# A four-tap convolution whose newest tap is written by ScalarE from the projection's bank

## The chip, the cores and the metric

The kernel runs on one core of a Trainium2 chip. The metric is the time of one execution on the device in microseconds; a kernel is given by the median of its runs. Two lengths are used: the time of a run, and the span of its profile from the first to the last instruction.

## The reference

The input is x of 32 sequences, 256 positions and 256 features, and a context of 120 keys for each sequence. Six blocks follow one another, each as x = layernorm(x + block(x)): random features, cross attention over the context with 16 heads, a gated rotation network with three cycles, a state space block, a gated product with the context, and a router over 8 experts. The state space block is the one that the change touches:

```python
xr = x @ W_in.T
x_ssm, res = (xr[..., :inner], xr[..., inner:])          # inner = 512
xc = jnp.pad(jnp.transpose(x_ssm, (0, 2, 1)), ((0, 0), (0, 0), (K - 1, 0)))
xc = lax.conv_general_dilated(xc, conv_w, (1,), 'VALID', feature_group_count=inner, ...)   # K = 4
x_conv = silu(jnp.transpose(xc, (0, 2, 1)) + conv_b)
delta = softplus(x_conv)
A_d = jnp.exp(delta[..., None] * -jnp.exp(A_log))         # 16 states
h = a_t * h + bx_t[..., None]; y = c_t * jnp.sum(h, axis=-1)   # over the sequence, bx = x_conv ** 2
return (y_ssm * silu(res) + D * x_conv) @ W_out.T
```

The convolution is depthwise and causal: output position s is the sum over k = 0 to 3 of conv_w[k] times input position s - 3 + k. Tap k = 3 is the newest one; it reads the position itself and needs no padding.

## The kernel before

The 32 sequences go in 16 groups of two (G = 16, NB = 2), that is 512 positions on the free axis. Three groups are in work at a time. In one turn of the loop the function `turn` (TensorE) or `turn_` (the other engines) does the front of group f (attention, then the rotation network), the state space block of group m = f - 1, the back of group b = f - 2 (gated product, router, experts), and prepares f + 1. The order of instructions on every engine is written out by hand, and each engine works through its own list strictly in that order; semaphores tie the lists together. Fifteen turns have both an f and an m, 14 of them a b too; in the last turn with an m there is no f.

The state space block starts with a projection of 1024 outputs in 8 chunks of 128 (`mamba_in`). TensorE writes chunks 0, 2, 4 and 7 to bank 4, chunks 1, 3 and 5 to bank 5, chunk 6 to bank 7 (`IN`). Chunks 0 to 3 are the convolution's input, chunks 4 to 7 are `res`. TensorE mixes the chunks with other work in this order: chunks 0 and 1, the queries of f, chunk 2, scores 0, chunk 3, scores 1, the turned x of b, chunk 4, scores 2, the gated product's input, scores 3, chunk 5, scores 4, chunk 6, scores 5 to 7, chunk 7, and then the attention itself. The scores rotate over three banks, and two groups of them stand in front of VectorE's maxima at the most: a group waits for the semaphore `smax_ready` of the group before it.

ScalarE (`mamba_in`, L1437) copies each of chunks 0 to 3 from its bank to `xpad`, a tile in SBUF with three zero columns ahead of each sequence, and raises `in_read`; TensorE waits for `in_read` before it fills a bank again. ScalarE's order around this is: the turned x of f and m, chunks 0 and 1, the queries of f, chunks 2 and 3, the turned x of b (`x45T`), a load of the silu table, silu of convolution chunks 0 and 1, softplus of them, six decays, silu of chunks 2 and 3, and then `res` (L1440).

VectorE computes the convolution from `xpad` in two calls (`convolve(m, 0)` and `convolve(m, 2)`), two chunks each. A call waits for both of its chunks. Tap 0 is a TENSOR_SCALAR (L1064), which writes `conv`; taps 1 to 3 are SCALAR_TENSOR_TENSOR (L1066), which add to it. The two chunks alternate, so that an instruction waits for the one before the last. VectorE's order is: the norm of b, `convolve(m, 0)`, four maxima of the scores (L991), `convolve(m, 2)`, twelve maxima, and then the scans (L1087) with everything else between them. The tile `conv` is the same memory as `soft` and `delta`: softplus is written over it, GpSimd adds to it (L1658), and ScalarE's 64 decays (L1479) read it.

GpSimd adds up the 16 states of each chunk (L1671) while VectorE scans.

Of the kernel before, what the change touches and what calls it, by code (L numbers as in the profile page):

```python
# [21 lines left out]
ALU = mybir.AluOpType  # L22
ACT = mybir.ActivationFunctionType
# [3 lines left out]
B, S, D = 32, 256, 256  # L27
# [10 lines left out]
INNER, STATES, TAPS = 512, 16, 4  # L38
IC = INNER // P
# [97 lines left out]
def program(nc, ins, out):  # L137
    nc.disable_value_cache = True
    with ExitStack() as ctx:
        def sb(name, shape, dt=F32):  # L140
            return ctx.enter_context(nc.sbuf_tensor(name, shape, dt))

        def sem(name, per=1, head=0):
            return Signal(ctx.enter_context(nc.semaphore(name)), per, head)

        def chain(name, per):
            return Chain(ctx.enter_context(nc.semaphore(name)), per)
# [6 lines left out]
        def col(name, k=0, rows=P):  # L154
            at = COLUMNS[name][0] + k
            return W["columns"][0:rows, at:at + 1]
# [70 lines left out]
        xpad = sb("xpad", [P, IC, NB, PAD + S])  # L227
# [3 lines left out]
        conv = delta = soft  # L231
# [108 lines left out]

        in_psum = sem("in_psum", 2 * IC)
        in_read = sem("in_read", 2 * IC)
        conv_chain = chain("conv_chain", IC * (TAPS - 1))
        conv_ready = sem("conv_ready", IC)
        xc_ready = sem("xc_ready", IC)
        exp_ready = sem("exp_ready", IC)
# [84 lines left out]
        IN = [bank[k][:, :] for k in (4, 5, 4, 5, 4, 5, 7, 4)]  # L431
# [101 lines left out]
        def _(pe):  # L533
            def mm(o, l, r, start, stop):
                return pe.matmul(o, l, r, start=start, stop=stop)  # L535
# [188 lines left out]
            def mamba_in(g, b, j0, j1):  # L724
                if j0 == 0:
                    if g == 0:
                        pe.wait_ge(loaded_rest.sem, 16 * len(REST))
                    pe.wait_ge(n3.xT_ready.sem, n3.xT_ready.at(g, DC))
                for j in range(j0, j1):
                    if j == IC + 2:  # L730
                        if b is not None:
                            pe.wait_ge(n4.xT_ready.sem, n4.xT_ready.at(b, DC))
                    elif j >= 2:
                        pe.wait_ge(in_read.sem, in_read.at(g, IC + 1 if j == 2 * IC - 1 else j - 1))
                    for c in range(DC):
                        last = mm(IN[j], winT[:, c, j * P:(j + 1) * P], n3.xT[:, c, :], c == 0, c == DC - 1)
                    last.then_inc(in_psum.sem, 1)
# [80 lines left out]
            def turn(f, m, b, nxt):  # L818
# [7 lines left out]
                if m is not None:  # L826
                    norm_turn(pe, n3, m, TURN)
                    mamba_in(m, b, 0, 2)
                if f is not None:
                    queries(f)  # L830
                if m is not None:
                    mamba_in(m, b, 2, 3)
                if f is not None:
                    scores(f, 0, 1)
                if m is not None:
                    mamba_in(m, b, 3, 4)
# [100 lines left out]
        def _(v):  # L937
# [113 lines left out]
            def convolve(g, c0):  # L1051

                if c0 == 0:
                    conv_chain.start(v, g)
                v.wait_ge(in_read.sem, in_read.at(g, c0 + 2))
                for k in range(TAPS):
                    for c in range(c0, c0 + 2):
                        o = conv[:, c, :].rearrange("p (b s) -> p b s", b=NB)
                        x = xpad[:, c, :, k:k + S]
                        w = col("conv_w", c * TAPS + k)  # L1060
                        if k:
                            conv_chain.settle(1)
                        if k == 0:
                            step = v.tensor_scalar(o, x, w, None, ALU.mult)  # L1064
                        else:
                            step = v.scalar_tensor_tensor(out=o, in0=x, scalar=w, in1=o, op0=ALU.mult,  # L1066
                                                          op1=ALU.add)
                        if k < TAPS - 1:
                            conv_chain.then(step)
                        else:  # L1070
                            step.then_inc(conv_ready.sem, 1)
                            if c == c0:
                                conv_chain.settle()
                if c0 + 2 == IC:
                    conv_chain.end()
# [147 lines left out]
            def turn_(f, m, b, nxt):  # L1223
# [4 lines left out]
                if m is not None:  # L1228
                    convolve(m, 0)
                if f is not None:  # L1230
                    maxima(f, 0, 2)
                if m is not None:
                    convolve(m, 2)
# [103 lines left out]
        def _(a):  # L1337
# [95 lines left out]
            def mamba_in(g, j0, j1):  # L1433
                for j in range(j0, j1):
                    a.wait_ge(in_psum.sem, in_psum.at(g, j + 1))
                    if j < IC:
                        a.copy(xpad[:, j, :, PAD:PAD + S], IN[j].rearrange("p (b s) -> p b s", b=NB))\  # L1437
                            .then_inc(in_read.sem, 1)
                    else:
                        a.activation(res[:, j - IC, :], IN[j], ACT.Silu).then_inc(in_read.sem, 1)  # L1440
# [68 lines left out]
            def turn_(f, m, b, nxt):  # L1509
# [7 lines left out]
                if m is not None:  # L1517
                    mamba_in(m, 0, 2)
                if f is not None:
                    queries(f)  # L1520
                if m is not None:
                    mamba_in(m, 2, IC)
# [250 lines left out]
```

## Time and profile before

| | before |
|---|---|
| median of 3 runs | 3107.59 us |
| lowest and highest run | 3103.23 and 3112.39 us |
| the profiled execution, its time | 3099.29 us |
| the profiled execution, its span | 3097.5 us |
| TensorE busy (matmul) | 2540.1 us, 82% |
| VectorE busy | 2495.3 us, 81% |
| ScalarE busy | 1727.8 us, 56% |
| GpSimd busy | 1487.4 us, 48% |
| mean granted clock of TensorE | 0.872 |

Names in the profile: PE is TensorE's matmuls, PEld its weight loads, DVE VectorE, ACT ScalarE, POOL GpSimd. A line L1066 is line 1066 of the kernel; `mm` is a helper at L535, so nearly all matmuls bear that line and are told apart by their tiles. Times in a timeline are microseconds from the start of the span. A timeline merges neighbouring instructions of one form: "x2" is two instructions, and the length beside it is that from the start of the first to the end of the last. Two neighbours overlap a little, so two of 0.59 us can take 1.07 us. The brackets at a row's end give the engine's idle time before it and what ended it.

### The profile page before, as it was taken

Reading aid. Unit: us, or ns where it says so; the run is one execution under the profiler, and the core shown is the slowest. Engines: PE = TensorE matmul, PEld = TensorE weight load, DVE = VectorE, ACT = ScalarE, POOL = GpSimd, SP = SyncE. Lnnn points to the kernel's source line nnn. Section 1 sums busy time; section 2 is a strip of 40 time slices with the busy share of each in tenths; the row PEclk is TensorE's granted clock in tenths of the full one; section 3 lists DMA queues with packets and bytes.
Section 4 is the critical chain, followed back from the end, with each engine's and each line's share of the span. In section 5 each row is a group of like instructions: output and inputs, shape, how many; then the busy total and the mean of one; then the engine's idle time right before and its main releaser. Section 6 shows DMA issues by size and latency. Waiting matters only on the chain.

```text
span 3097.5 us, 41602 instructions
## 1 busy us (share of the span) xinstructions
PE 2540.1 (82%) x11020; PEld 1469.9 (47%) x11020; DVE 2495.3 (81%) x4288; ACT 1727.8 (56%) x3062; POOL 1487.4 (48%) x1159
## 2 busy tenths in 40 slices
PE   6896888979888897888988788888888889887556
PEld 3544554544444454445545444554544445454323
DVE  2368888897978889898888978788897888978783
ACT  1457564646657474665646466564656646465620
POOL 1046354554535455563545545354553545456460
PEclk7868888888989989999898899898898989978687
DMA  3000000000000000000000000000000000000000
GB/s 131 10 8 10 14 11 14 17 14 7 10 21 10 14 17 14 7 10 21 10 14 13 18 7 10 21 10 14 13 3 21 10 14 7 7 7 1 14 7 7
DMA packets 16849, 45.72 MB, mean 15 GB/s; under 512 B 2248, under 2 KB 7056, under 8 KB 16400
## 3 DMA queue, kind: packets, MB, share of 16 engines
q1 hardware_dynamic: 16656, 43.96, 4.2%
q14 instruction: 171, 1.40, 0.2%
q8 instruction: 22, 0.36, 0.1%
HBM read 35.57 MB, written 8.39 MB: 14 GB/s over the span
## 4 chain that ended last, share of the span: by engine, by line
PE 47%; DVE 28%; issue 14%; ACT 7%; DVEq 2%; POOL 1%; ACTq 0%; DMA 0%; SPq 0%; POOLq 0%
PE bank L535 45%; DVE h_ring L1087 14%; DVE x L1199 3%; DVE ln_stats L387 2%; DVE smax L991 1%; POOL ysum L1671 1%; ACT a_ring L1479 1%; DVE x L405 1%; DVE xpad L1093 1%; PE bank L413 1%; DVE soft L1066 1%; ACT L1485 1%; ACT L1339 1%; DVE ln_mv L391 1%; ACT spare L1420 1%
## 5 line engine op out<-in xcount | busy, mean ns | idle before, releaser
L1671 POOL TENSOR_TENSOR ysum<-ysum,h_ring 128x512 f32<-128x512 f32 x896 | 1155.2, 1289 | 633.3 <-DVE h_ring L1087 571.3
L1087 DVE TENSOR_TENSOR_SCAN h_ring<-a_ring,bank 128x512 f32<-128x512 f32 x1024 | 1172.7, 1200 | 27.2 <-ACT bank L1474 16.2
L1479 ACT ACTIVATE a_ring<-soft,decay 128x510 f32<-128x510 f32 x1024 | 675.7, 717 | 198.4 <-DVE h_ring L1087 198.0
L535 PE MATMUL bank<-w_expert_w,x45T 128*128 128x512 f32 x1024 | 541.1, 675 | 199.0 <-DVE x L1199 191.4
L535 PEld LDWEIGHTS bank<-w_expert_w,x45T 128*128 128x128 f32 x1024 | 213.2, 216 | 490.9 <-DVE x L1199 253.5
L1658 POOL TENSOR_TENSOR soft<-xc,soft 128x512 f32<-128x512 f32 x64 | 81.0, 1276 | 655.2 <-ACT soft L1457 655.2
L535 PE MATMUL bank<-x3T,w_winT 128*128 128x512 f32 x512 | 291.0, 704 | 39.7 <-ACT x3T L419 31.4
L991 DVE TENSOR_REDUCE smax<-bank 128x4 f32<-128x480 f32 x256 | 156.4, 652 | 143.1 <-PE bank L535 143.1
L535 PE MATMUL bank<-qT,kmask 32*120 32x256 f32 x1024 | 207.2, 497 | 50.2 <-ACT spare L1386 40.6
L535 PE MATMUL bank<-spare,w_cn_w 128*128 128x256 f32 x768 | 217.7, 408 | 37.0 <-ACT spare L1416 22.4
L1199 DVE SCALAR_TENSOR_TENSOR x<-bank,weight,x 128x256 f32<-128x256 f32 x512 | 212.5, 474 | 40.4 <-PE bank L535 40.4
L398 ACT ACTIVATE ln_logv<-ln_mv,eps 128x4 f32<-128x4 f32 x96 | 28.3, 295 | 330.5 <-DVE ln_mv L391 252.7
L535 PE MATMUL bank<-kmask,qT 32*128 32x240 f32 x1024 | 151.8, 417 | 46.1 <-DVE smax L991 45.2
L1386 ACT ACTIVATE spare<-bank 120x512 f32<-120x512 f32 x256 | 138.4, 593 | 81.5 <-PE bank L535 81.4
L535 PEld LDWEIGHTS bank<-x3T,w_winT 128*128 128x128 f32 x512 | 104.3, 220 | 165.1 <-issue 111.5
L535 PEld LDWEIGHTS bank<-spare,w_cn_w 128*128 128x128 f32 x768 | 131.8, 193 | 105.7 <-ACT spare L1416 37.3
L535 PE MATMUL bank<-x12T,w_cn_w 128*128 128x256 f32 x768 | 180.0, 384 | 2.3 <-ACT x12T L1372 2.3
L1671 POOL TENSOR_TENSOR ysum<-h_ring 128x512 f32<-128x512 f32 x64 | 81.3, 1270 | 197.5 <-DVE h_ring L1087 197.5
L413 PE MATMUL bank<-w_ident,x 128*128 128x128 f32 x640 | 127.4, 322 | 49.6 <-DVE x L405 45.6
L535 PEld LDWEIGHTS bank<-x12T,w_cn_w 128*128 128x128 f32 x768 | 146.0, 192 | 40.3 <-issue 20.1
L1416 ACT ACTIVATE spare<-bank,w_columns 128x256 f32<-128x256 f32 x192 | 80.5, 472 | 139.6 <-PE bank L535 139.3
L535 PEld LDWEIGHTS bank<-kmask,qT 32*128 32x128 f32 x1024 | 94.9, 198 | 129.5 <-DVE smax L991 83.8
(149 smaller groups left out, 3890.2 us busy)
## 6 DMA issues: line engine op xcount, KB each, us to landing
x0T<-in_xT SPq DMA_DIRECT2D x16, 512.0 KB, 3.3
x<-in_x SPq DMA_DIRECT2D x16, 512.0 KB, 4.3
out<-x SPq DMA_DIRECT2D x16, 512.0 KB, 3.0
ctxT<-in_ctxT SPq DMA_DIRECT2D x16, 240.0 KB, 2.5
ctxTb<-in_ctxT SPq DMA_DIRECT2D x16, 240.0 KB, 2.7
ctxb<-in_ctx SPq DMA_DIRECT2D x16, 240.0 KB, 3.0
w_expert_w<-in_expert_w SPq DMA_DIRECT2D x1, 2048.0 KB
w_winT<-in_winT SPq DMA_DIRECT2D x1, 1024.0 KB
```

The lines of the kernel that those rows point to most:

```text
L387: n.chain.then(v.bn_stats(n.stats[:, t, :], n.sum[:, t, :]))
L391: last = v.bn_aggr(n.mv[:, t, :], n.stats[:, t, :])
L413: last = pe.transpose(banks[c][:, t * P:(t + 1) * P], n.x[:, t, c * P:(c + 1) * P], ident[:, :])
L535: return pe.matmul(o, l, r, start=start, stop=stop)
L991: v.tensor_reduce(smax[:, t, :].rearrange("p (e r h) -> p r e h", e=DC, r=4)[:, r, :, :], bank[u % 3][:, 0:480].rearrange("p (e h k) -> p ...
L1087: scanned.then(v.tensor_tensor_scan(h_ring[:, k % HRING, :], a_ring[:, k % RING, :, :].rearrange("p b s -> p (b s)"), xc2, 0.0, ALU.mult, ...
L1199: v.scalar_tensor_tensor(out=acc[:, t, :], in0=MB[s % 2][:, e * D:(e + 1) * D], scalar=weight[:, t, x:x + 1], in1=acc[:, t, :], op0=ALU.mu ...
L1386: a.activation(probs[:, s % 4, :, :].rearrange("p k s -> p (k s)"), bank[s % 3][0:KEYS, :], ACT.Exp, scale=1.0 / np.sqrt(DK)).then_inc(pro ...
L1416: a.activation(h1[:, b, r, :], bank[b][:, r * S:(r + 1) * S], ACT.Gelu, bias=col("cn_b1", r)).then_inc(l1_ready.sem, 1)
L1479: a.activation(a_ring[:, k % RING, :, 1:S], delta[:, c, :].rearrange("p (b s) -> p b s", b=NB)[:, :, 1:S], ACT.Exp, scale=decay[:, k:k + 1 ...
L1658: p.tensor_tensor(out=delta[:, c, :], in0=xc[:, c, :], in1=soft[:, c, :], op=ALU.add)\
L1671: p.tensor_tensor(out=total, in0=first, in1=h_ring[:, k % HRING, :], op=ALU.add)\
```

## The change

For chunks 0 to 3 ScalarE issues two reads of the bank instead of one. The first is new: it multiplies the bank by the weight of tap 3 (a column of 128 weights, one for each partition) and writes the result to the convolution's tile, raising the new semaphore `tap_ready`. The second is the copy to `xpad`, as before. VectorE waits for both, and adds taps 0, 1 and 2 with SCALAR_TENSOR_TENSOR; its TENSOR_SCALAR is gone. TensorE waits for `tap_ready` beside `in_read` before it fills a bank again. The taps are added in another order.

```diff
-        conv_chain = chain("conv_chain", IC * (TAPS - 1))
+        conv_chain = chain("conv_chain", IC * (TAPS - 2))
+        tap_ready = sem("tap_ready", IC)
...
                         pe.wait_ge(in_read.sem, in_read.at(g, IC + 1 if j == 2 * IC - 1 else j - 1))
+                        pe.wait_ge(tap_ready.sem, tap_ready.at(g, min(j - 1, IC)))
...
                 v.wait_ge(in_read.sem, in_read.at(g, c0 + 2))
-                for k in range(TAPS):
+                v.wait_ge(tap_ready.sem, tap_ready.at(g, c0 + 2))
+                for k in range(TAPS - 1):
                     for c in range(c0, c0 + 2):
                         o = conv[:, c, :].rearrange("p (b s) -> p b s", b=NB)
-                        x = xpad[:, c, :, k:k + S]
-                        w = col("conv_w", c * TAPS + k)
                         if k:
                             conv_chain.settle(1)
-                        if k == 0:
-                            step = v.tensor_scalar(o, x, w, None, ALU.mult)
-                        else:
-                            step = v.scalar_tensor_tensor(out=o, in0=x, scalar=w, in1=o, op0=ALU.mult,
-                                                          op1=ALU.add)
-                        if k < TAPS - 1:
+                        step = v.scalar_tensor_tensor(out=o, in0=xpad[:, c, :, k:k + S],
+                                                      scalar=col("conv_w", c * TAPS + k), in1=o, op0=ALU.mult,
+                                                      op1=ALU.add)
+                        if k < TAPS - 2:
                             conv_chain.then(step)
...
                     if j < IC:
+                        a.activation(conv[:, j, :], IN[j], ACT.Copy, scale=col("conv_w", j * TAPS + TAPS - 1))\
+                            .then_inc(tap_ready.sem, 1)
                         a.copy(xpad[:, j, :, PAD:PAD + S], IN[j].rearrange("p (b s) -> p b s", b=NB))\
                             .then_inc(in_read.sem, 1)
```

## Rows read from the trace of the kernel before

**Rows 1.** Page: busy time of each engine; the chain that ended last, by engine.

```profile
PE 2540.1 (82%) x11020; PEld 1469.9 (47%) x11020; DVE 2495.3 (81%) x4288; ACT 1727.8 (56%) x3062; POOL 1487.4 (48%) x1159
...
PE 47%; DVE 28%; issue 14%; ACT 7%; DVEq 2%; POOL 1%; ACTq 0%; DMA 0%; SPq 0%; POOLq 0%
```

**Rows 2.** Timeline of VectorE: start of the first convolution in two turns.

```profile
333.43 0.89 DVE L1064 TENSOR_SCALAR soft<-xpad,w_columns 128x512 f32<-128x512 f32 x2 [1.54 <-ACT xpad L1437]
...
2694.54 0.89 DVE L1064 TENSOR_SCALAR soft<-xpad,w_columns 128x512 f32<-128x512 f32 x2 [1.16 <-ACT xpad L1437]
```

**Rows 3.** Timeline of VectorE, one turn, both halves of the convolution.

```profile
1238.63 0.89 DVE L1064 TENSOR_SCALAR soft<-xpad,w_columns 128x512 f32<-128x512 f32 x2 [2.04 <-ACT xpad L1437]
1239.43 4.06 DVE L1066 SCALAR_TENSOR_TENSOR soft<-xpad,w_columns,soft 128x512 f32<-128x512 f32 x6
1244.16 1.22 DVE L991 TENSOR_REDUCE smax<-bank 128x4 f32<-128x480 f32 x2 [0.67 <-PE bank L535]
...
1248.23 0.87 DVE L1064 TENSOR_SCALAR soft<-xpad,w_columns 128x512 f32<-128x512 f32 x2
1249.02 4.06 DVE L1066 SCALAR_TENSOR_TENSOR soft<-xpad,w_columns,soft 128x512 f32<-128x512 f32 x6
1252.99 1.21 DVE L991 TENSOR_REDUCE smax<-bank 128x4 f32<-128x480 f32 x2
```

**Rows 4.** Timeline of TensorE: same turn; two rows of the first turn.

```profile
1241.24 1.88 PE L535 MATMUL bank<-x3T,w_winT 128*128 128x512 f32 x4
...
1244.06 1.98 PE L535 MATMUL bank<-x3T,w_winT 128*128 128x512 f32 x4
...
1253.70 1.08 PE L535 MATMUL bank<-kmask,qT 32*128 32x240 f32 x8 [0.97 <-DVE smax L991]
...
1263.19 1.97 PE L535 MATMUL bank<-kmask,qT 32*128 32x240 f32 x8 [0.74 <-DVE smax L991]
1265.09 3.78 PE L535 MATMUL bank<-x3T,w_winT 128*128 128x512 f32 x4
...
181.57 1.97 PE L535 MATMUL bank<-kmask,qT 32*128 32x240 f32 x8 [3.81 <-DVE smax L991]
```

**Rows 5.** Chain that ended last, same turn: start, length, what.

```profile
1234.27 12.83 PE bank L535 x40
...
1253.08 0.58 DVE smax L991
```

**Rows 6.** Groups by line and form: busy, mean ns; idle before, releaser.

```profile
L1066 DVE SCALAR_TENSOR_TENSOR soft<-xpad,w_columns,soft 128x512 f32<-128x512 f32 x192 | 129.9, 745 | 0.0
L1064 DVE TENSOR_SCALAR soft<-xpad,w_columns 128x512 f32<-128x512 f32 x64 | 28.1, 482 | 52.7 <-ACT xpad L1437 52.7
...
L1378 ACT ACTIVATE qT<-bank,w_columns 128x512 f32<-128x512 f32 x32 | 22.0, 688 | 37.2 <-PE bank L535 37.2
```

**Rows 7.** Timeline of ScalarE, same turn.

```profile
1238.01 0.59 ACT L1437 COPY xpad<-bank 128x512 f32<-128x512 f32 x1 [1.13 <-PE bank L535]
1239.73 0.69 ACT L1378 ACTIVATE qT<-bank,w_columns 128x512 f32<-128x512 f32 x1 [1.13 <-PE bank L535]
...
1246.08 0.59 ACT L1437 COPY xpad<-bank 128x512 f32<-128x512 f32 x1 [2.34 <-PE bank L535]
1247.68 1.08 ACT L419 COPY x45T<-bank 128x512 f32<-128x512 f32 x2 [1.01 <-PE bank L413]
...
1262.63 1.55 ACT L1440 ACTIVATE res<-bank 128x512 f32<-128x512 f32 x3
1268.90 0.60 ACT L1440 ACTIVATE res<-bank 128x512 f32<-128x512 f32 x1 [4.73 <-PE bank L535]
```

**Rows 8.** Timeline of ScalarE, last turn with a convolution.

```profile
2882.50 1.08 ACT L419 COPY x45T<-bank 128x512 f32<-128x512 f32 x2
```

**Rows 9.** Stretches: length, busy time of engines, granted clock, DMA share, GB/s.

```profile
1264.00:1266.00 2.00, 2.00 (x7) 0.93 (x6) 0.81 (x2) 0.17 (x1) 0.00 (x0) 0.50 0.00 0
```

**Rows 10.** Timeline of TensorE: chunks 0 and 1 in another turn.

```profile
693.74 6.78 PE L535 MATMUL bank<-x3T,w_winT 128*128 128x512 f32 x8 [2.49 <-ACT x3T L419]
```

## The prediction

> **What bounds the kernel now.** I read the page first. TensorE and VectorE are both busy a little over 80% of the span, ScalarE 56%, and the chain of work that ended last runs 47% over TensorE and 28% over VectorE, 7% over ScalarE [rows 1]. So no engine is full from end to end: the end is set by a path that changes engines, and a microsecond counts only where that path passes. I then took one turn of the loop out of the middle (1234 to 1414 us) and laid the engines' timelines beside each other. Fifteen turns have this shape (a group in the convolution stage and one in the score stage together); from the first convolution at 333.43 us to that at 2694.54 us there are 13 turn lengths, so 181.6 us each [rows 2].
>
> The convolution stands twice in a turn, and its two halves are unlike. The first half starts at 1238.63 us, when ScalarE has copied chunk 1, and ends at 1243.49; VectorE then idles 0.67 us for TensorE's first scores [rows 3]. The second half starts at 1248.23 us with no idle before it, ends at 1253.08, and the maxima behind it start at once [rows 3]. TensorE stands still for 0.97 us before the scores of 1253.70, and is released by the first of those maxima [rows 4]. The chain says the same: it goes straight through the second half, its first maximum and into TensorE, while at the first half it is on TensorE, one piece of 12.83 us [rows 5]. This release is in all 15 turns: 14 show a wait of 0.97 to 1.06 us at this place, the first turn one of 3.81 us [rows 4]. The last convolution (2879 us) has no scores beside it.
>
> **What is removed.** Four TENSOR_SCALAR in a turn (64 in all, 482 ns each) [rows 6]. What they take from VectorE is their step from start to start: in each half the pair starts at 1238.63 and the next form at 1239.43, so 0.80 us; in the second half 1248.23 to 1249.02, so 0.79 us [rows 3]. The six SCALAR_TENSOR_TENSOR of a half stay, 4.06 us. It is not a quarter of the half that goes: a quarter of 4.86 us would be 1.21 us. The tap that goes is the cheap kind (482 ns against 745 ns) [rows 6]. The Trainium skill has this rule (VectorE: DVE Perf Modes, "The perf-mode tier table"): a single-source fp32 operation in SBUF streams two elements per cycle, one with two tensor sources only one. By it the change takes the wrong tap away, and the trace agrees; a reader who counted taps as equal would get 15 x 1.21 = 18.2 us where I count 15 x 0.80.
>
> **What is added.** 64 scaled copies on ScalarE, out of the bank into the convolution's tile. No row shows this form. Nearest is a read of the bank with a column operand, 688 ns (L1378) [rows 6]; a plain copy from the bank takes 0.59 us (L1437) [rows 7]. Neighbours overlap: two plain copies of about 0.59 take 1.08 us together, a step of 0.49 us [rows 7]. So the new instruction moves the copy behind it by 0.49 us if it is as cheap as a plain copy, and by 0.69 if it costs as much as L1378 and nothing overlaps; I take 0.59, the length of L1378, which has the same source and a column operand too, less the 0.10 of overlap. That is 64 x 0.59 = 38 us more for ScalarE, and the question is only what waits behind it:
> - Chunk 1: bank full at 1238.01, both reads done at 1238.01 + 0.59 + 0.59 = 1239.19 instead of 1238.60. ScalarE next acts at 1239.73, when TensorE hands over the queries, after 1.13 us idle [rows 7]; 0.54 us are left. VectorE starts its first half 0.59 later and is 0.80 shorter: it ends 0.21 us earlier than now and waits 0.88 instead of 0.67 us for TensorE. Gain here: nothing.
> - Chunk 3: both reads done at 1246.08 + 1.18 = 1247.26. VectorE wants chunk 3 at 1248.23, ScalarE's next work (x45T) comes from TensorE at 1247.68 after 1.01 us idle [rows 7]. Both are still in time, by 0.97 and 0.42 us.
> - TensorE's new wait (tap_ready, in front of chunks 2 to 7) comes with in_read, which stays the later one: the copy stands behind the scaled copy in ScalarE's order. Chunks 0 and 1 are read by 1239.2, and TensorE refills those banks from 1241.24 and 1244.06 [rows 4]. Chunk 2 is complete at 1241.24 + 1.88 = 1243.12 and read by 1244.3; its bank is refilled only by chunk 4, behind chunk 3, which itself ends at 1246.04. So the wait is free, by 1.7 us or more. What stands behind this wait in TensorE's queue are the scores, so it would be dear if it were late.
> - No DMA, no GpSimd work and no table load is added or moved.
>
> **The sum.** Only the second half is on the path. Its maxima come 0.79 us earlier, at 1252.20; the first ends near 1252.87 and TensorE could go on at 1252.91 instead of 1253.70. It is free from 1252.73 (its wait was 0.97), so the whole 0.79 passes; the bounds are 0 and 0.97. Then: TensorE alternates scores and projections up to chunk 7 at 1265.09. That one needs ScalarE's first read of res, 1262.63 + 0.60 = 1263.23, which is not moved by the change; wanted at 1264.30, so 1.07 us are left [rows 4, 7]. ScalarE then idles 4.73 us for chunk 7 [rows 7], and softmax, scans and GpSimd's sums all hang on it, so they move along. Fifteen turns x 0.79 = 11.9 us.
>
> In the last turn ScalarE is the path: chunk 3 is copied at 2882.01 and x45T follows without idle at 2882.50, then silu, softplus and decays [rows 8]. There the scaled copy of chunk 3 costs its 0.59 us. Net 11.9 - 0.6 = 11.3 us. The profiled execution took 3099.29 us (span 3097.5), so it would be 3088.0; the median of the three runs is 3107.59, 8.3 above it. The difference taken from the median gives 3107.59 - 11.3 = **3096.3 us**, 0.36% less. A difference of 0.3%, 9.3 us, is about the least that can be told from none here, so the forecast lies close to that line.
>
> **Rivals.**
> - **The clock trades the gain for a loss; slower.** The granted clock is 0.50 of 2.4 GHz, that is 1.2, in the score stage from 1264 to 1266, after pauses of TensorE [rows 4, 9]. Where such low stretches lie differs from turn to turn. The dear place is the start of the stage: the chain's one piece from chunk 0 to the first maximum is 12.83 us in 8 of 15 turns and 14.4 to 15.9 in the other 7, because the first two chunks run at the low clock there, 6.78 us in the one shown [rows 5, 10]. The 7 together lose 15.9 us. A shorter turn shifts all stretches. If all 15 started at the low clock, at 3.0 us each, that is 45 - 15.9 = 29 us more, and 3107.6 - 11.3 + 29 = 3125 us; it is a loss from 11.3 us on, that is four further turns. For it: the spread of the rows. Against it: nothing ties the stretches to the turn, so they should scatter as before. Chance 0.08.
> - **The clock stays up; much faster.** In the score stage chunk 7 takes 3.78 us at the low clock, chunk 3 with the same four instructions 1.98 at full clock [rows 4]. If 0.79 us less idling kept the clock up, 15 x 1.8 = 27 us more would go: 3069 us. The Trainium skill (TensorE: Matmul & The Clock Gate, "What's actually happening") has the engine's own recent activity release the throttle; by that rule less idling can only help, and 3069 us is what it would give at best. Against it: the two waits of 0.74 us directly before the fall remain as they are [rows 4]. Chance 0.09, mostly for a part of it.
> - **The time is lost again within the turn; no change.** A release that I could not see (ScalarE's order, a sum of GpSimd, chunk 7) takes the 0.79 us. Least slack has chunk 7's read of res, 1.07 us; if that is gone, 0 to 0.4 us per turn stay: 3102 to 3107.6, say 3105. The weight of VectorE's scans, which run nearly without idle, speaks against it: they also start 0.79 earlier. Chance 0.18.
> - **The form is dearer than its neighbours; no change or slower.** From a step of 1.56 us on (1248.23 - 1246.08 - 0.59) the second half starts late. At 2 us it is 0.44 late and 0.35 of 0.79 are left: 15 x 0.35 - 2 = 3.3 us, 3104. Chance 0.03.
>
> **How the numbers follow.** The forecast has 0.62. The three runs of before spread from 3103.2 to 3112.4, so a median moves by some 4 us and a difference of two by some 6; around 3096.3 about two thirds of it lie beyond 3098.3. Its own range is 3088 to 3104. Faster by over 0.3%: 0.62 x 0.68 + 0.09 = 0.51, and a little of the third case, 0.53. Slower by over 0.3%: 0.08. The rest, 0.39, is within 0.3%. The range for 8 in 10 takes in part of the clock rivals on either side and the whole of the third: 3083 to 3111 us.
>
> **What would show it.** In the profile after: 64 TENSOR_SCALAR fewer on VectorE, 64 scaled copies of about 0.69 us on ScalarE; the first maximum of the third pair about 3.97 us after the second half's start instead of 4.76; the wait of 0.97 before the fourth group of scores down to about 0.2; VectorE's idle before the first half up by 0.6 and its wait for the first scores from 0.67 to about 0.9; turns of 180.8 us on average at the same mean clock (0.872). I am wrong if ScalarE's idle before the queries or x45T is used up, if TensorE waits for ScalarE at chunk 7, or if the mean granted clock moves by more than 0.005.

## The result and the profile after

The changed kernel is slower: median 3131.43 us of 9 runs (3117.99 to 3139.41) against 3106.93 us for the kernel before, measured beside it in 9 runs, ratio 1.0086, 95% interval 1.0066 to 1.0105. The forecast was 3096.3, 35 us lower. The profiled execution took 3120.36 us (span 3118.5), where before's took 3099.29.

The page of the kernel after, busy times and the chain by engine, to be held against [rows 1]:

```profile
PE 2563.2 (82%) x11020; PEld 1473.6 (47%) x11020; DVE 2469.8 (79%) x4224; ACT 1765.0 (57%) x3126; POOL 1487.2 (48%) x1159
...
PE 46%; DVE 25%; issue 16%; ACT 7%; POOL 3%; DVEq 2%; ACTq 0%; DMA 0%; POOLq 0%; SPq 0%
```

VectorE has 64 instructions and 26 us less, ScalarE 64 more. TensorE has the same 11020 matmuls, and 23 us more busy time: the same work at a lower granted clock (mean 0.868, before 0.872). In the chain VectorE's share falls by 3 points, and "issue", time in which an engine waits for nothing that the profile shows, rises by 2.

The part that the change aims at came as forecast. Timelines of the kernel after in one turn, of VectorE, of ScalarE and of TensorE, against [rows 3], [rows 7] and [rows 4]:

```profile
1260.30 1.22 DVE L993 TENSOR_REDUCE smax<-bank 128x4 f32<-128x480 f32 x2 [0.79 <-PE bank L536]
1263.22 1.22 DVE L993 TENSOR_REDUCE smax<-bank 128x4 f32<-128x480 f32 x2 [1.70 <-PE bank L536]
1264.36 4.05 DVE L1064 SCALAR_TENSOR_TENSOR soft<-xpad,w_columns,soft 128x512 f32<-128x512 f32 x6
1268.34 1.21 DVE L993 TENSOR_REDUCE smax<-bank 128x4 f32<-128x480 f32 x2
```

```profile
1251.32 0.69 ACT L1436 ACTIVATE soft<-bank,w_columns 128x512 f32<-128x512 f32 x1 [3.44 <-PE bank L536]
1251.90 0.58 ACT L1438 COPY xpad<-bank 128x512 f32<-128x512 f32 x1
```

```profile
1269.04 1.08 PE L536 MATMUL bank<-kmask,qT 32*128 32x240 f32 x8 [0.18 <-DVE smax L993]
```

The second half runs from 1264.36 to 1268.34, 3.98 us instead of 4.76. The scaled copy takes 0.69 us and moves the copy behind it by 0.58. TensorE's wait ahead of the fourth scores is 0.18 us where it was 0.97. So the loss is elsewhere. Two other places show it.

**TensorE and its code.** The page lists the queues by which the engines fetch their instructions. First the kernel before, then the kernel after: queue, packets, MB, share.

```profile
q14 instruction: 171, 1.40, 0.2%
q8 instruction: 22, 0.36, 0.1%
```

```profile
q8 instruction: 67, 1.10, 0.2%
q14 instruction: 171, 1.40, 0.2%
```

q8 went from 22 to 67 packets of 16 KB: 9 more in each of five turns. In these turns TensorE stops in a run of transposes that has nothing to wait for. Timeline of TensorE, kernel after, across the jump back to the loop's head:

```profile
1225.27 5.75 PE L536 MATMUL bank<-w_woutT,xpad 128*128 128x256 f32 x24
1230.86 0.60 PE L720 MATMUL bank<-w_ident,x12T 128*128 128x128 f32 x4
1232.47 0.32 PE L720 MATMUL bank<-w_ident,x12T 128*128 128x128 f32 x1 [1.01 <-issue]
1235.25 0.55 PE L720 MATMUL bank<-w_ident,x12T 128*128 128x128 f32 x3 [2.45 <-issue]
1235.63 2.94 PE L536 MATMUL bank<-w_woutT,xpad 128*128 128x256 f32 x8
...
1247.50 6.61 PE L536 MATMUL bank<-x3T,w_winT 128*128 128x512 f32 x8 [5.71 <-ACT x3T L420]
```

In before the same eight transposes are one row of 1.04 us. Here they take 4.94 us.

**ScalarE at the start of a turn.** Timeline of ScalarE, the first copies behind the jump back; before, then after:

```profile
1411.94 1.07 ACT L419 COPY x12T<-bank 128x512 f32<-128x512 f32 x2 [2.45 <-PE bank L413]
1412.90 0.60 ACT L419 COPY x3T<-bank 128x512 f32<-128x512 f32 x1
1414.09 0.59 ACT L419 COPY x3T<-bank 128x512 f32<-128x512 f32 x1 [0.58 <-issue]
```

```profile
1425.30 0.59 ACT L420 COPY x12T<-bank 128x512 f32<-128x512 f32 x1 [2.80 <-issue]
1427.30 0.59 ACT L420 COPY x12T<-bank 128x512 f32<-128x512 f32 x1 [1.41 <-issue]
1427.78 1.08 ACT L420 COPY x3T<-bank 128x512 f32<-128x512 f32 x2
```

From the first to the end of the last of the four copies it was 2.74 us; it is 3.56, with a second pause of 1.41 us inside. TensorE needs x3T for chunk 0. View of waits (engine, place, releaser: us in total, times, longest), before and after:

```profile
PE bank L535 <- ACT x3T L419: 31.4, 16, 2.9
```

```profile
PE bank L536 <- ACT x3T L420: 47.2, 16, 5.7
```

Laid out by stage, from TensorE's timelines, mean of the same 13 turns of the profiled executions (us; a turn runs from chunk 0 to chunk 0; "low" is the sum of the stretches with granted clock 0.5 in the whole span):

| kernel | chunks 0, 1 | queries to 4th scores | middle | turn's end | turn | low |
|---|---|---|---|---|---|---|
| before | 4.61 | 15.89 | 151.19 | 9.94 | 181.63 | 795 |
| after | 5.64 | 15.09 | 150.19 | 12.59 | 183.52 | 826 |

"Turn's end" is from the transposes back (L719, L720) to chunk 0. The 0.80 us are gained in the second column; the third gains 1.0; the fourth, where both pauses lie, loses 2.65, and the first, chunks 0 and 1, loses 1.03: they run at the low clock, wholly or in part, in 14 of 15 turns instead of 7. 13 x 1.89 = 24.6 us.

### The profile page after: what moved, and what is told of

It reads as the page before. It is cut to its first block, busy times and chain, and to the rows that moved or that the text cites. A ratio compares the mean times of both kernels' runs of the same rounds, so it can differ in the third digit from the quotient of the medians.

```text
span 3118.5 us, 41662 instructions
## 1 busy us (share of the span) xinstructions
PE 2563.2 (82%) x11020; PEld 1473.6 (47%) x11020; DVE 2469.8 (79%) x4224; ACT 1765.0 (57%) x3126; POOL 1487.2 (48%) x1159
## 3 DMA queue, kind: packets, MB, share of 16 engines
HBM read 35.57 MB, written 8.39 MB: 14 GB/s over the span
## 4 chain that ended last, share of the span: by engine, by line
PE 46%; DVE 25%; issue 16%; ACT 7%; POOL 3%; DVEq 2%; ACTq 0%; DMA 0%; POOLq 0%; SPq 0%
PE bank L536 45%; DVE h_ring L1086 12%; POOL ysum L1672 3%; DVE x L1198 3%; DVE ln_stats L388 2%; ACT a_ring L1480 1%; DVE smax L993 1%; DVE soft L1064 1%; DVE x L406 1%; PE bank L414 1%; DVE xpad L1092 1%; ACT L1486 1%; DVE ln_mv L392 1%; ACT L1338 1%; ACT spare L1419 0%
## 5 line engine op out<-in xcount | busy, mean ns | idle before, releaser
L536 PE MATMUL bank<-w_expert_w,x45T 128*128 128x512 f32 x1024 | 531.7, 665 | 205.5 <-DVE x L1198 197.9
L1064 DVE SCALAR_TENSOR_TENSOR soft<-xpad,w_columns,soft 128x512 f32<-128x512 f32 x192 | 129.8, 746 | 78.6 <-ACT xpad L1438 78.6
L536 PE MATMUL bank<-kmask,qT 32*128 32x240 f32 x1024 | 145.4, 403 | 34.2 <-DVE smax L993 33.3
```

Source lines behind the costliest of these rows:

```text
L1064: step = v.scalar_tensor_tensor(out=o, in0=xpad[:, c, :, k:k + S], scalar=col("conv_w", c * TAPS + k), in1=o, op0=ALU.mult, op1=ALU.add)
```

## The experiments

Theories. **A:** the added instructions (in a turn TensorE's five waits, not six, as chunk 6 has none, and ScalarE's four copies) move the code, and an engine fetches its code at other places or more often. **B:** the change's own work and waits cost the time. **C:** the turn shortened by 0.8 us lies differently among the stretches at the low clock, and that costs time. **D:** ScalarE's added copies or the added waits do so. Paddings are empty instructions (an increment of a semaphore that nobody waits for), run once, ahead of the loop: they move the loop's code and add nothing to a turn. A label's before_ or after_ says which kernel was edited; short_both is an edit of the kernel before, one_sem_both of the changed one.

The kernels ran in four lots on four chips, 4 to 10 runs each, with the kernel before beside every lot: its medians are 3107.95 us (first four kernels), 3101.82 (next four, to before_pe5), 3105.93 (next four) and 3104.13 (last two). Ratios are to the kernel before of the same lot; a difference between two lots carries up to 6 us of the chips' own.

**TensorE's padding.**

```
@@ TensorE, the changed kernel @@
+            for _ in range(16):
+                pe.sem_inc(held.sem, 1)
             turn(0, None, None, 1)
```

> The changed kernel with 16 empty instructions (increments of an unused semaphore) on TensorE ahead of the turns, so that its loop stands 16 instructions further on; nothing in the loop differs. Theory A (place of the code): the changed kernel's TensorE queue loads code again in 5 of its turns (67 packets on the instruction queue q8 against 22), each with pauses of 2 to 3 us before the rotated chunks are turned back (19.3 us on TensorE in total) and some 4 us longer; with another place the packets fall back to about 22 and the time by 15 to 25 us, from 3131 to about 3110. ScalarE's pauses stay. Theory B (the added reads and waits cost by themselves, or low clock stretches fell badly): no change of the packets that matters, 3125 to 3137.

Measured (after_pe16): 3106.69 us (3103.34 to 3112.29), ratio to before 1.0008 (0.9990 to 1.0026); q8 has 22 packets again and the stops in the transposes are gone. The turn's end goes from 12.59 to 10.94 us. Against the changed kernel's 3131.4 that is 25 us for 16 empty instructions: A.

**ScalarE's padding.**

```
@@ ScalarE, the changed kernel @@
+            for _ in range(8):
+                a.sem_inc(held.sem, 1)
             feat(0, 0)
```

> The changed kernel with 8 empty instructions on ScalarE ahead of the turns; nothing in the loop differs. Theory A: in the changed kernel ScalarE stands still twice at each jump back, once for 2.5 to 2.9 us, and again for about 2.0 us three instructions later, between its two copies of x12T; the first copies of a turn are late, TensorE idles longer before chunk 0 and starts it at the low clock in 13 of 15 turns. Eight instructions further on the second pause is gone (x12T waits on issue fall from 50.8 to about 25 us in total), the slow starts become fewer, and the time falls by 25 to 40 us, to 3091 to 3106, the 5 turns with TensorE's loading staying. Theory B: ScalarE's pauses are not on the path or not tied to the place: 3125 to 3137.

Measured (after_act8): 3096.90 us (3089.00 to 3102.83), ratio 0.9964 (0.9949 to 0.9978). q14 falls from 171 to 111 packets, so 60 of its packets brought ScalarE's code, 5 at each of 12 jumps; q8 has 49 here, 27 more than 22, 9 in each of three turns. No pause of ScalarE for "issue" is left, neither the new one nor the old one of before.

**Both paddings, on the changed kernel and on the kernel before.** The edits are the two above together.

> The changed kernel with both paddings (16 on TensorE, 8 on ScalarE). Theory A: both gains, 3131 - 20 - 33 = about 3078, between 3068 and 3092. Theory B: 3125 to 3137.

> The kernel before with the same two paddings: the partner of the run above, so that their difference is the work alone. Theory A: ScalarE's second pause of the kernel before (about 1.05 us, seven instructions after the jump) goes too, 13 x 0.5 to 1 us, so 3090 to 3103; and the changed kernel with paddings is 9 to 15 us faster than this one, which is the sum of the forecast (11.3 us) once the place of the code is taken out. Theory B: this stays at 3107, 20 us or more below the changed kernel with paddings.

Measured: after_both 3083.07 us (3080.94 to 3086.00), ratio 0.9920 (0.9888 to 0.9951), as expected. before_both 3053.86 us (3053.10 to 3055.66), ratio 0.9827 (0.9796 to 0.9858), some 40 us below what I expected. Where neither TensorE nor ScalarE pauses for "issue", the kernel before gains 54 us, the changed kernel 48, and **the change costs 29 us**, where by its own work it should gain 12. Code isn't all of it.

Stretches of the first 3.5 us of chunk 0 in successive turns (from:to, length, then busy time of the engines, granted clock, DMA share, GB/s); before_both, then after_both:

```profile
862.33:865.83 3.50, 3.50 (x8) 1.62 (x9) 2.75 (x11) 0.98 (x3) 0.00 (x0) 1.00 0.71 263
1041.36:1044.86 3.50, 3.50 (x4) 1.51 (x5) 2.75 (x11) 0.50 (x2) 0.00 (x0) 0.50 0.86 284
1219.27:1222.77 3.50, 3.50 (x8) 1.63 (x9) 2.75 (x11) 0.98 (x3) 0.00 (x0) 1.00 0.75 261
1395.86:1399.36 3.50, 3.50 (x4) 1.51 (x5) 2.75 (x11) 0.50 (x2) 0.00 (x0) 0.50 0.87 300
1577.19:1580.69 3.50, 3.50 (x4) 1.51 (x5) 2.75 (x11) 0.50 (x2) 0.00 (x0) 0.50 0.83 302
1755.07:1758.57 3.50, 3.50 (x8) 1.63 (x9) 2.60 (x10) 0.98 (x3) 0.00 (x0) 1.00 0.76 253
```

```profile
869.76:873.26 3.50, 3.50 (x4) 1.50 (x5) 2.42 (x10) 0.50 (x2) 0.00 (x0) 0.50 0.84 298
1050.78:1054.28 3.50, 3.50 (x4) 1.50 (x5) 2.67 (x10) 0.50 (x2) 0.00 (x0) 0.50 0.84 300
1231.75:1235.25 3.50, 3.50 (x4) 1.50 (x5) 2.51 (x10) 0.50 (x2) 0.00 (x0) 0.50 0.86 298
1412.74:1416.24 3.50, 3.50 (x4) 1.51 (x5) 2.57 (x10) 0.50 (x2) 0.00 (x0) 0.50 0.84 286
1593.77:1597.27 3.50, 3.50 (x4) 1.51 (x5) 2.67 (x10) 0.50 (x2) 0.00 (x0) 0.50 0.88 300
```

The stretches begin where chunk 0 begins, so the distance of two is a turn. In before_both the turns last 179.0, 177.9, 176.6, 181.3, 177.9 us, and some begin at 2.4 GHz (1.00) and some at 1.2 (0.50). In after_both each lasts 181.0 us and begins at 0.50: the turn has locked to the low stretches, and stays so to the end of the loop, 12 turns of 181.0 or 180.9 us in all.

**The shortening alone.** The kernel before with both paddings, and VectorE's first step left out (the first tap's product is missing); nothing is added on ScalarE or TensorE.

```
@@ convolve, the kernel before @@
-                for k in range(TAPS):
+                for k in range(1, TAPS):
...
-                        if k == 0:
-                            step = v.tensor_scalar(o, x, w, None, ALU.mult)
-                        else:
-                            step = v.scalar_tensor_tensor(out=o, in0=x, scalar=w, in1=o, ...)
+                        step = v.scalar_tensor_tensor(out=o, in0=x, scalar=w,
+                                                      in1=xpad[:, c, :, 0:S] if k == 1 else o, ...)
```

> The kernel before with both paddings (16 empty instructions ahead of TensorE's loop, 8 ahead of ScalarE's; 3053.9 us), with VectorE's first step of the convolution left out: the second step takes a slice of the padded input in the place of the first step's product. Part of the computation is changed: the first tap's product is missing. ScalarE does nothing more than in the kernel before, and there is no added wait. VectorE's half of the convolution is 0.8 us shorter, as in the changed kernel. Theory C (the shortened turn falls in with the stretches at the low clock, so that the shortening itself costs time): near the changed kernel with both paddings, 3070 to 3090 us, with every turn's chunks 0 and 1 at the low clock. Theory D (what the changed kernel adds, ScalarE's scaled copies and the waits on tap_ready, costs the 29 us): 3036 to 3054 us, up to 15 x 0.8 = 12 us faster than 3053.9.

Measured (short_both): 3086.31 us (3080.68 to 3088.74), ratio 0.9952 (0.9936 to 0.9967). Work is only taken away, and the kernel is 32 us slower than before_both. Theory D isn't needed for the loss, and C forecast it. That the way goes through the clock and not through VectorE's own code, which is shortened too, is looked at below.

**The added work with the time of the old step given back.**

```
@@ convolve, the changed kernel @@
+                for c in range(c0, c0 + 2):
+                    v.tensor_scalar(xc[:, c, :]..., xpad[:, c, :, 0:S], col("conv_w", c * TAPS), None, ALU.mult)
                 for k in range(TAPS - 1):
```

> The changed kernel with both paddings (3083.1 us) and, ahead of the three steps of each half of the convolution, two TENSOR_SCALARs of VectorE of the old form whose products are overwritten unread by the SiLU's output. All that the change adds is in it, and the old first step's time is back: work is only added. Theory C (the shortening costs the time): near the kernel before with both paddings, 3050 to 3068 us, 15 to 30 us faster than without the added steps. Theory D (the added copies and waits cost the time): 3083 + 15 x 0.8 = 3095 us or a little less, 3080 to 3098.

Measured (after_both_ts): 3049.54 us (3040.92 to 3056.17), ratio 0.9825 (0.9790 to 0.9861), the same as before_both. Four instructions more in each turn than after_both, and 33 us less. All that the change adds, copies and waits, costs nothing that can be seen: its copies are covered, as forecast. In these three turns the starts of chunk 0 repeat those of before_both within half a microsecond:

```profile
862.83:866.33 3.50, 3.50 (x8) 1.63 (x9) 2.69 (x10) 1.43 (x4) 0.00 (x0) 1.00 0.77 257
1041.81:1045.31 3.50, 3.50 (x4) 1.50 (x5) 2.75 (x11) 0.50 (x2) 0.00 (x0) 0.50 0.87 290
1219.70:1223.20 3.50, 3.50 (x8) 1.63 (x9) 2.69 (x10) 1.43 (x4) 0.00 (x0) 1.00 0.77 263
```

**The waits taken out.**

```
@@ the changed kernel: tap_ready is dropped, the scaled copy counts on in_read @@
-        tap_ready = sem("tap_ready", IC)
-        in_read = sem("in_read", 2 * IC)
+        in_read = sem("in_read", 3 * IC)
...
-                            .then_inc(tap_ready.sem, 1)
+                            .then_inc(in_read.sem, 1)
```

> The changed kernel with both paddings, and with ScalarE's scaled copy counted on in_read itself, in the place of a semaphore tap_ready of its own: TensorE's six and VectorE's two added waits of a turn are gone, ScalarE's added copies stay. TensorE's loop has then again the length of the kernel before. Theory C (the shortened turn and the clock): 3075 to 3090 us, as with tap_ready (3083.1). Theory D in its form that the waits cost the time: near 3042 to 3056 us, since the copies are covered and the turn is 0.8 us shorter.

Measured (one_sem_both): 3085.93 us (3084.38 to 3089.70), no faster than with tap_ready. The waits taken out are five of TensorE in a turn, not six. By themselves they cost nothing here; the turn is the locked one again, 180.64 us.

**Half of the time given back, and more than all of it.** One such TENSOR_SCALAR in the second half of the changed kernel; two more in the second half of the kernel before.

```
@@ convolve @@
+                if c0:
+                    for c in range(c0, c0 + 1):      # c0 + 2 in the kernel before
+                        v.tensor_scalar(xc[:, c, :]..., xpad[:, c, :, 0:S], col("conv_w", c * TAPS), None, ALU.mult)
```

> The changed kernel with both paddings (3083.1 us) and one TENSOR_SCALAR of the old form (0.40 us) ahead of the steps of VectorE's second half, its product overwritten unread. Theory C (the turn's place among the stretches at the low clock sets the time): no proportion to the work; either the turns stay locked, 3079 to 3088 us, with all turns' chunks 0 and 1 at the low clock, or the lock breaks as with the full 0.8 us, 3040 to 3062. Theory L (the time follows the length of the turn, one way or the other, in proportion): half way between the kernels with none and with all of the added work, (3083 + 3050) : 2 = 3066 us, or, if added work only adds, 3083 + 15 x 0.4 = 3089.

> The kernel before with both paddings (3053.9 us) and two more TENSOR_SCALARs (0.8 us together) ahead of the steps of VectorE's second half, their products overwritten unread: a turn 0.8 us longer than before's, as the changed kernel's is 0.8 us shorter. Theory L (work only adds): 3054 + 15 x 0.8 = 3066 us, 3062 to 3070. Theory C (place among the low stretches): anything from 3040 to 3085 us, and a mean turn that differs from 178.15 + 0.8 = 178.95 us by more than 0.5 us, with the difference in the stages behind the convolution and in how many turns begin at the low clock.

Measured: after_both_ts1 3083.63 us (3078.95 to 3084.18): half of the time buys nothing, and 12 of 15 turns begin low. before_both_ts2 3100.04 us (3090.64 to 3109.93), against 3066 by the length: the 0.8 us cost 46 (38 between the two profiled executions), above the range that I gave C too. Only 4 of its turns begin low; its losses lie in the middle of the turn. The padded kernels by stage, as in the table above:

| kernel | chunks 0, 1 | queries to 4th scores | middle | turn's end | turn | low | median |
|---|---|---|---|---|---|---|---|
| short_both | 5.31 | 15.09 | 151.87 | 8.35 | 180.63 | 833 | 3086.3 |
| one_sem_both | 5.31 | 15.09 | 151.88 | 8.35 | 180.64 | 847 | 3085.9 |
| after_both | 5.52 | 15.09 | 151.89 | 8.39 | 180.90 | 840 | 3083.1 |
| after_both_ts1 | 5.00 | 15.49 | 151.37 | 8.38 | 180.23 | 829 | 3083.6 |
| after_both_ts | 4.53 | 15.89 | 149.58 | 8.15 | 178.15 | 775 | 3049.5 |
| before_both | 4.52 | 15.89 | 149.59 | 8.15 | 178.15 | 771 | 3053.9 |
| before_both_ts2 | 4.02 | 16.68 | 152.05 | 8.34 | 181.09 | 802 | 3100.0 |

The second column follows the work exactly, in steps of 0.4 and 0.8 us. The rest does not. after_both has 69 us more at the low clock than before_both; at half speed the same work loses half of that, 34 us, and 29 + 12 (the gain that doesn't arrive) = 41 us are missing. So by this estimate the clock has most of it; the last 7 us I can't place.

VectorE's own code is the rival to C. Its turn, too, is shorter (560 instructions from jump to jump in after_both, 566 in before_both), and in 12 turns of a shortened kernel it pauses for "issue" at the turn's start, 11.3 us in all in after_both and 16.0 in short_both. In after_both_ts1 it is 5.4 us, at the same time of the kernel. No padding of VectorE was run, but the rows show what the pause costs. VectorE in after_both, the pause and the convolution that follows:

```profile
1231.99 1.43 DVE L1116 BATCH_NORM_STATS2 ln_stats<-bank 128x6 f32<-128x256 f32 x4 [1.01 <-issue]
...
1238.96 4.07 DVE L1066 SCALAR_TENSOR_TENSOR soft<-xpad,w_columns,soft 128x512 f32<-128x512 f32 x6 [2.51 <-ACT xpad L1440]
```

Behind each of the 12 pauses of after_both VectorE idles 2.4 to 2.8 us more for ScalarE's copy of chunk 1, so the pause is covered. And before_both, which has no such pause above 0.43 us, has slow turns as well. Two of its turns, then one of after_both (columns as above):

```profile
1395.86:1577.19 181.33, 157.17 (x688) 90.57 (x688) 155.55 (x266) 107.68 (x191) 92.78 (x72) 0.89 0.04 13
1577.19:1755.07 177.88, 152.74 (x688) 88.37 (x689) 155.23 (x266) 107.34 (x191) 92.78 (x72) 0.91 0.04 13
```

```profile
1231.75:1412.74 180.99, 157.64 (x688) 90.65 (x688) 154.11 (x262) 109.87 (x195) 92.79 (x72) 0.89 0.04 13
```

In before_both the same work takes 3.45 us more in the turn with the lower clock, and TensorE is busy 4.4 us longer. The locked turn of after_both is such a turn, one after the other, where before_both has a mixture. What makes a turn of this length fall into it each time, and whether VectorE's pause has a part in that, stays open.

**The moved code alone, TensorE.**

```
@@ TensorE, the kernel before, behind the wait on in_read @@
+                        pe.sem_inc(held.sem, 1)
```

> The kernel before with five empty instructions of TensorE more in each turn of the loop, one behind each of the chunks' waits on in_read; nothing waits for what they count. Theory A (place and length of the code): TensorE's code is loaded anew in several turns, as in the changed kernel (67 packets of the code queue in the place of 22, pauses of 3 us and more ahead of the rotation back), and the kernel is 10 to 25 us slower than the kernel before, 3117 to 3132 us. Theory B (the change's own added work): five empty instructions of some 0.05 us cost 15 x 0.25 = 4 us at most, 3107 to 3111 us, 22 packets.

Measured (before_pe5): 3138.49 us (3125.86 to 3159.88), ratio 1.0135 (1.0076 to 1.0194), 76 packets on q8. The stops in the transposes are back:

```profile
PE bank L719 <- issue: 25.1, 12, 3.0
```

In the kernel after this row of the waits is 19.3 us in 10; the kernel before has none.

**The moved code alone, ScalarE.**

```
@@ ScalarE, mamba_in, the kernel before @@
                     if j < IC:
+                        a.sem_inc(held.sem, 1)
                         a.copy(xpad[:, j, :, PAD:PAD + S], ...
```

> The kernel before with four empty instructions of ScalarE more in each turn, one ahead of each of chunks 0 to 3's copies, as the changed kernel has four scaled copies more there. Nothing else is changed. Theory A (the place of ScalarE's code): a second pause of about 2 us between the two first x12T copies of a turn, which moves the turn's first chunk later by about 2 us; with it 3107 to 3132 us, slower than the kernel before by up to 15 x 1.6 = 24. Theory B (the empty instructions themselves): 15 x 0.2 = 3 us at most, 3104 to 3110, without such a pause.

Measured (before_act4): 3130.03 us (3127.63 to 3132.81), ratio 1.0089 (1.0057 to 1.0121). Four empty instructions in a turn give what the whole change gave. Waits of ScalarE for "issue" at the x12T copies; before, after, and this kernel:

```profile
ACT x12T L419 <- issue: 25.7, 10, 2.7
```

```profile
ACT x12T L420 <- issue: 50.8, 24, 3.7
```

```profile
ACT x12T L419 <- issue: 49.0, 24, 2.8
```

24 times in place of 10: two pauses in each of 12 turns.

**ScalarE's padding alone on the kernel before.** The edit of after_act8, on the kernel before.

> The kernel before with ScalarE's padding alone (8 empty instructions ahead of its loop). Theory A (ScalarE's wait for its code at each turn's start is on the path): 3054 to 3075 us, with 111 packets of the engines' code queue and ScalarE's first instruction 0.3 us behind the jump; if TensorE's padding has no part in before_both's gain, since TensorE loads no code anew in either, within 6 us of 3053.9. Theory E (the 54 us came from TensorE's padding or from both together): 3090 to 3108 us.

Measured (before_act8): 3047.01 us (3043.09 to 3051.20), ratio 0.9820 (0.9788 to 0.9853), the fastest kernel here beside after_both_ts. TensorE's padding has no part in before_both's gain. TensorE's wait for x3T falls to a third of before's 31.4 us:

```profile
PE bank L535 <- ACT x3T L419: 11.1, 16, 0.8
```

The turn's end is shorter by 1.79 us (8.15 for 9.94), 27 us in fifteen turns, and 20 of them are this wait. The middle is shorter by 1.9 (149.30 for 151.19), with 44 us less at the low clock (751 for 795). Together they are 55 of the 59 us.

**What each cause has in the changed kernel as it stands.** Two kernels without paddings: the kernel before with both kinds of empty instructions in the loop (before_pe5 and before_act4 together), and the changed kernel with the old first step's time given back (as after_both_ts).

> The kernel before with the empty instructions of both: five more of TensorE and four more of ScalarE in each turn, where the changed kernel has its added waits and copies. Theory F (the moved code by itself explains the changed kernel's loss, and the shortened turn gives back a little or nothing): 3125 to 3145 us, 67 packets on TensorE's code queue and the second pause of ScalarE in every turn. Theory G (the losses add, and the shortened turn gives back most in this setting): 3107 + 30 + 24 = 3160 us or more, at least 3150. Theory H (the shortened turn is the larger part of the loss here too): 3100 to 3115.

> The changed kernel without paddings, and with the two TENSOR_SCALARs of the old form ahead of each half's steps, their products overwritten unread: only the time of the old first step is given back. Theory F: within 10 us of the changed kernel's 3131, 3121 to 3141. Theory G (here the shortening gains as on paper or more): 3131 + 15 x 0.8 = 3143 us or more, 3140 to 3160. Theory H (the shortening costs here as it does with the paddings, 29 us): 3100 to 3112.

Measured: before_pe5_act4 3152.86 us (3145.96 to 3175.00), ratio 1.0183 (1.0142 to 1.0225). after_ts 3147.47 us (3130.26 to 3160.81), ratio 1.0156 (1.0127 to 1.0186). Theory G is the nearest. The code of TensorE and ScalarE as long as in the changed kernel, without its work, costs 49 us; the change itself takes 24 of them back. Given back its time, it loses 19 (43 instead of 24.5 us over before). So at this place the shorter turn gains 19 to 24 us by the medians. The runs spread widely (31 and 29 us over four), and the intervals of the ratios stand only 7 and 11 us apart: that there is a gain is shown, that it is more than the 12 us of the work is not. Without the pauses for code it loses 29. The two losses of single engines don't add (37 and 24 alone, 49 together); in the profiled executions TensorE's code was loaded anew in six turns of before_pe5 and in three of before_pe5_act4 (76 and 49 packets).

## Why the prediction was wrong

- **What bounds the kernel, and what is removed.** Right: only the second half of the convolution is on the path, and 0.80 us of each turn went, in the stage forecast (15.89 to 15.09). TensorE's wait is 0.18 where "about 0.2" was said; VectorE's wait for the first scores 0.79 where 0.9 was said.
- **What is added.** The form costs what its neighbour costs, 688 ns, and moves the copy by 0.58 where 0.59 was taken. Chunks 1 and 3 were read in time: nothing that follows them starts late in the turn shown. The rival of the dearer form is out.
- **The step that failed** is the list of what is added: "So the wait is free" and "No DMA, no GpSimd work and no table load is added or moved". The waits are free as waits, but they are instructions, five in TensorE's turn and four copies in ScalarE's, and the code is brought by queues of its own. The page's section on queues had them (22 and 171 packets), and the waits view had ScalarE's 25.7 us for "issue" at the turn's start. I had both before me and weighed neither. The term for the moved code was missing from the sum; before_pe5_act4 measures it: +49 us by the medians, 44 to 70 by the interval of the ratio. The Trainium skill (Runtime: NRT & Kernel Launch, "Instruction fetch mechanics") says that a taken branch to a page that isn't loaded stops the engine until it is fetched. The rows fit that, 2.4 to 2.9 us behind nearly every jump on ScalarE. The same section calls the ordinary crossing of a block mostly hidden; whether the second pause, the 1.41 us inside a turn's first copies, is such a crossing or a part of the jump's fetch, no run here shows.
- **The sum 15 x 0.79 = 11.9 us** is no bound either way. With TensorE's and ScalarE's code equally long, the same 0.8 us per turn brought a gain of 24 us (before_pe5_act4 against after), and a loss of 29 (before_both against after_both).
- **The slower rival** had its end right and half of its mechanism: in 14 turns of 15 chunks 0 and 1 do run at the low clock, wholly or in part, and it gave 3125. Its chance of 0.08 rested on "nothing ties the stretches to the turn, so they should scatter as before". That is the second step that failed. They can be tied: 12 successive turns of after_both last 181.0 or 180.9 us and begin in the same low stretch. And the rival alone doesn't explain the kernel after: chunks 0 and 1 lose 1.03 us a turn, 15 us, which the middle stages give back, and the 2.65 us at the turn's end lie where both engines pause for "issue". That its 3125 came near is luck.
- **The faster rival** took from the Trainium skill (TensorE: Matmul & The Clock Gate, "What's actually happening"), by which the engine's own recent activity releases the throttle, that less idling can only help. In short_both TensorE idles 506 us of the span, in before_both 512, and yet short_both spends 833 us at the low clock instead of 771. So the step from recent activity to the idling of the whole kernel doesn't hold here, and the measurement decides; the page's sentence itself is not refuted by it.
- **What I said would show me wrong** did not: no idle time of ScalarE was used up, TensorE doesn't wait for it at chunk 7, and the mean clock moved by 0.004. The signs covered the terms of my sum, not a term that it lacked.

## What to carry to other kernels

Before costing an edit of a kernel with a loop, read the page's rows of the code queues and the "issue" rows of the waits at the loop's head, and count the instructions that the edit adds on every engine, waits too: here four empty ones cost 24 us, and eight put ahead of the loop gained 59, five times what the edit was to bring. Test the place of the code with a padding before judging an edit of under 1%; a comparison of two kernels with different code lengths measures both. And where the clock moves within a turn, measure an edit at several lengths of the turn: 0.8 us less per turn came out as 29 us lost (before_both to after_both), 24 gained (before_pe5_act4 to after) and 46 gained (before_both_ts2 to before_both).

## What was not expected of the hardware

- At each of 12 jumps back ScalarE began 2.4 to 2.9 us late, once 3.7 (kernels before and after). With its loop moved by 8 instructions it begins 0.24 us behind the jump, and q14 brings 60 packets of 8 KB fewer (1.40 MB in 171 before). Why this place is a good one and the one 8 instructions earlier isn't, no run here settles.
- TensorE's code is loaded anew (9 packets of 16 KB) in some turns and not in others of one execution, once its loop is five instructions longer: q8 has 67, 76, 49 and 49 packets in four kernels with it (after, before_pe5, after_act8, before_pe5_act4), and 22 in after_ts, which has it too. Sixteen empty instructions ahead of the loop end it. What sets the turn in which it happens is open.
- A turn can lock to the stretches at the low clock: 180.9 to 181.0 us, turn after turn, in after_both and short_both, and for most turns still with 0.4 us of work more. With 0.8 us more it unlocks, and the mean turn falls to 178.15 us. With 0.8 us more again it is 181.1, without a steady lock: the turns last from 176.8 to 184.3, though seven of the 13 last 181.0 to 181.4. Each series of turns is that of one profiled execution.
